# Five projections of a four-layer transformer stack computed with tokens on partitions, their gates multiplied into the weights, and the setup and three orders rearranged

## What is computed

```python
x = x + (cross_attention(ada_ln(x, cond), ctx) @ Wp + bp)              # L0, 64 context keys
x = L1(x)   # evidence attention, router over 3 experts, gate, out_w
# L2
x = x + gate_a * (self_attention(modulate(ln(x))) @ W_proj + b_proj)   # 1024 keys
x = x + (cross_attention(x @ W_qc, ctx) @ W_cproj + b_cproj)
x = x + gate_m * mlp(modulate(ln(x)))                                  # gelu, 1024 hidden
# L3
x = x + gate_sa * (window_attention(modulate(ln(x))) @ w_so + b_so)    # 8 windows of 128
x = x + gate_ca * (topk_attention(modulate(ln(x))) @ w_co + b_co)      # best 16 of 64 keys
x = x + gate_ml * swiglu(modulate(ln(x)))                              # 1024 hidden
```

## Time and profile before

| | us |
|---|---|
| median of 3 runs | 1692.78 |
| lowest, highest | 1691.51, 1701.95 |
| the profiled execution | 1699.16 |
| its span in the trace | 1697.3 |
| PE busy | 1538.0 (91%) |
| DVE busy | 1046.0 (62%) |
| ACT busy | 797.7 (47%) |
| POOL busy | 373.6 (22%) |

### The profile page before, as it was taken

The page is one execution under the profiler, slowest core; times in us unless marked ns, Lnnn a source line. Parts: engine busy times, 40 slices in busy tenths (PEclk is TensorE's granted clock), DMA queues, the critical chain, the costliest instruction groups (busy, mean ns, idle before and its releaser), DMA issues.

```text
span 1697.3 us, 26247 instructions
## 1 busy us (share of the span) xinstructions
PE 1538.0 (91%) x10421; PEld 908.9 (54%) x10421; DVE 1046.0 (62%) x2921; ACT 797.7 (47%) x1264; POOL 373.6 (22%) x418
## 2 busy tenths in 40 slices
PE   5889998999988998877988999899998999887888
PEld 3446564444343856546763657444444476655666
DVE  3363355899627445899357334489982634579953
ACT  1334421688844533335543443148886354233454
POOL 4510006332015110114142000433300600001330
PEclk9989999899999999999999899989999999999899
DMA  9300017221020000000220000632202000000000
GB/s 349 122 1 1 0 42 146 35 37 25 2 75 1 1 1 2 2 1 1 77 86 1 0 0 1 157 49 39 39 2 75 1 1 1 2 2 1 1 1 25
DMA packets 37650, 59.60 MB, mean 35 GB/s; under 512 B 7460, under 2 KB 27079, under 8 KB 36631
## 3 DMA queue, kind: packets, MB, share of 16 engines
q1 hardware_dynamic: 25239, 34.71, 6.1%
q0 software_dynamic: 9568, 15.87, 6.0%
q10 hardware_dynamic: 2720, 7.34, 1.2%
HBM read 42.03 MB, written 2.10 MB: 26 GB/s over the span
## 4 chain that ended last, share of the span: by engine, by line
PE 67%; DVE 17%; issue 6%; ACT 5%; SPq 3%; POOL 2%; DMA 1%; DVEq 0%; ACTq 0%; POOLq 0%
PE ps L963 9%; PE ps L456 9%; PE ps L975 8%; PE ps L1268 4%; PE ps L948 3%; PE ps L843 3%; PE ps L1057 3%; PE ps L1065 3%; DVE rs L2002 2%; PE ps L821 2%; PE ps L578 2%; PE ps L586 2%; DVE mxw L1994 2%; PE ps L1295 2%; DVE taken L2318 2%
## 5 line engine op out<-in xcount | busy, mean ns | idle before, releaser
L2188 DVE TENSOR_REDUCE mm<-ps 128x1 f32<-128x1024 f32 x256 | 310.1, 1223 | 38.7 <-PE ps L948 32.2
L1594 ACT ACTIVATE pt<-ps 128x512 f32<-128x512 f32 x512 | 276.6, 599 | 65.3 <-PE ps L963 47.9
L2430 POOL TENSOR_TENSOR rstd<-ve,minus_half 128x4 f32<-128x4 f32 x32 | 35.7, 1115 | 773.3 <-DVE ve L1881 773.3
L963 PE MATMUL ps<-qx,kx 64*128 64x512 f32 x512 | 192.4, 454 | 2.1 <-DMA qx<-mxT 1.2
L948 PE MATMUL ps<-kx,qx 48*128 48x512 f32 x512 | 191.3, 454 | 0.9 <-DVE mm L2188 0.7
L975 PE MATMUL ps<-pt,v 128*32 128x256 f32 x2048 | 162.4, 398 | 0.0
L963 PEld LDWEIGHTS ps<-qx,kx 64*128 64x128 f32 x512 | 80.8, 188 | 99.8 <-ACT pt L1594 86.4
L2078 DVE TENSOR_TENSOR rlo<-ring,rhi 128x512 fp32r<-128x512 f32 x48 | 33.2, 692 | 128.1 <-ACT ring L1545 128.0
L975 PEld LDWEIGHTS ps<-pt,v 128*32 128x32 f32 x2048 | 43.5, 110 | 88.5 <-ACT pt L1594 61.6
L948 PEld LDWEIGHTS ps<-kx,qx 48*128 48x128 f32 x512 | 77.4, 189 | 23.8 <-issue 15.4
L2476 POOL DMA_DIRECT2D qx<-mxT x64 | 33.0, 523 | 213.5 <-ACT mxT L1586 193.4
(11 more groups left out here) (353 smaller groups left out, 3391.9 us busy)
## 6 DMA issues: line engine op xcount, KB each, us to landing
wm<-in_L_xcond_W_mlp_dram SPq DMA_DIRECT2D x4, 1024.0 KB, 8.6
qx<-q_hi POOLq DMA_DIRECT2D x64, 64.0 KB, 2.6
kx<-k_hi POOLq DMA_DIRECT2D x64, 64.0 KB, 2.7
w3a<-in_L_xcond_w_m_dram SPq DMA_DIRECT2D x2, 2048.0 KB, 8.1
w<-in_L_xcond_e_w_dram SPq DMA_DIRECT2D x6, 512.0 KB, 7.1
w<-in_L_xcond_e_w_dram SPq DMA_DIRECT2D x2, 1536.0 KB, 11.9
s_ada<-in_L_xcond_w_ada_dram ACTq DMA_DIRECT2D x1, 2304.0 KB, 22.0
qx<-q_lo POOLq DMA_DIRECT2D x32, 64.0 KB, 2.5
```

The lines of the kernel that those rows point to most:

```text
L963: pe.matmul(ps[:, bank, :], kx[r, p % 4, kc * P:(kc + 1) * P], qx[r, p % 4, half * 512:(half + 1) * 512], start=True, stop=True).then_inc( ...
L1594: act.activation(pt[:, u % 8, half * 512:(half + 1) * 512], ps[:, bank, :], ACT.Exp, scale=QK_SCALE).then_inc(st_read, 1)
L2188: return dve.tensor_reduce(mm[:, p % 2, e, t:t + 1], place(), X, ALU.max).then_inc(ring_read, 1)
```

## The change

1. A new `projection` on PE makes a block's 512x256 output with tokens on partitions: two bias matmuls (f32r, a 64-partition broadcast column against `row_hl`, 512 columns) and eight fp32 matmuls of 256 columns, straight into the two banks that DVE adds to x. It replaces both parts of `residual` for i = 0, 2, 3, 5, 6; their ACT evictions go.
2. For i = 2, 5, 6 the gate is multiplied into the weight. In the L2 attention PE spreads the three gates over partitions (3 matmuls, banks 5 and 6), ACT copies them to `gates` behind both `high_parts(1, .)`, POOL multiplies wproj, wso and wco (128x512 each) after groups p = 1, 2, 3. PE waits for `gates_ready` at m == 16 (n == -6) of the lead, since the banks are needed again, and for `gates_in` before projection 2.
3. Setup: `load_x(0, 1)` goes right behind `load_x(0, 0)`; five row loads go from POOL to ACT's queue, ahead of the modulation weights; DVE makes statistics and xhat of block 0 after the scales, `s_ctxT`, the gates and 16 small copies into `s_cols`; PE makes the evidence products before the L0 keys and values; two transposes, a copy and a subtraction make `row_hl`, and the first `ln` waits for it (set_dve 14).
4. `kpair` moves to memory of its own and is made in the last MLP of the batch before; at the boundary the two halves of the block-1 query stand before and after `token_scores(0)`.
5. Window loop: DVE takes the maximum before the division, `ln(6, 0)` is at u == 13, `normalise(6, 0)` at u == 12.
6. L3: `up(2)` before `down(0)`, `hidden(2)` before `product_hi(1)`, `centre(6)` before `product_lo(0)`; some semaphores are merged.

```diff
+                def projection(row, k, w, src, bank, sources):
+                    column = row_of[:, N_ROW * b + row:N_ROW * b + row + 1].broadcast_to([64, P])
+                    for j in range(TB // 2):
+                        if j == 0 and sources[0] is not None:
+                            pe.wait_ge(*sources[0])
+                        pe.matmul(ps[:, bank + j, :], column, row_hl[:, :].unsqueeze(1).broadcast_to([64, 2, D]), start=True, stop=False)
+                    for c in range(KC):
+                        if sources[c + 1] is not None:
+                            pe.wait_ge(*sources[c + 1])
+                        for t in range(TB):
+                            ins = pe.matmul(ps[:, bank + t // 2, t % 2 * D:(t % 2 + 1) * D], src[:, k, c, t * P:(t + 1) * P], w[:, c, :],
+                                            start=False, stop=c == KC - 1 and t % 2 == 1)
+                            if c == KC - 1 and t % 2:
+                                ins.then_inc(y_turned, 1)
...
             load_x(0, 0)
+            load_x(0, 1)
...
             load_ra()
-            load_x(0, 1)
...
+            load_rows(act, 24, len(vectors), rows_ld[2])
...
-                residual(2, 0, False, wproj, src=hT, each=(hT_ready, b * 2 * N_HT + 12))
-                linear(6, wproj, 0, hT[:, 1], (hT_ready, b * 2 * N_HT + 14)).then_inc(y_done, 1)
-                residual(2, 0, True)
-                linear(7, wproj, 1, hT[:, 1]).then_inc(y_done, 1)
-                residual(2, 1, True)
+                pe.wait_ge(gates_in, b * 3 + 3)
+                h0 = b * 2 * N_HT + 12
+                projection(R_B_A, 0, wproj, hT, 2, (None, (hT_ready, h0 + 1), (hT_ready, h0 + 2)))
+                projection(R_B_A, 1, wproj, hT, 6, (None, (hT_ready, h0 + 3), (hT_ready, h0 + 4)))
...
                 pe.wait_ge(full_ready, b + 1)
+                for j in range(3):
+                    o = N_ROW * b + R_G_A + j
+                    ins = pe.matmul(ps[:, 5 + j // 2, j % 2 * D:(j % 2 + 1) * D], row_of[:, o:o + 1].broadcast_to([64, P]), row_hl[:, :], start=True, stop=True)
+                ins.then_inc(gates_spread, 1)
                 for n in range(-LEAD, UNITS):
                     (p, u), m = divmod(n, 2 * T), n + LEAD
                     q, at_m = divmod(m, 2 * T)
+                    if m == 2 * T:
+                        pe.wait_ge(gates_ready, b + 1)
...
                 for qk in range(2):
                     high_parts(1, qk)
+                act.wait_ge(gates_spread, b + 1)
+                act.activation(gates[:, 0:2, :], ps[:, 5, :].rearrange("p (j n) -> p j n", j=2), ACT.Copy)
+                act.activation(gates[:, 2, :], ps[:, 6, 0:D], ACT.Copy).then_inc(gates_ready, 1)
...
+                    if p in (1, 2, 3):
+                        if p == 1:
+                            pool.wait_ge(gates_ready, b + 1)
+                            pool.wait_ge(rc1_ld, b * 9 * 16 + 9 * 16)
+                            pool.sem_inc(passed, 1)
+                        w = (wproj, wso, wco)[p - 1]
+                        pool.tensor_tensor(w[:, :, :], w[:, :, :], gates[:, p - 1, :].unsqueeze(1).broadcast_to([P, KC, D]), ALU.mult).then_inc(gates_in, 1)
...
                     if led:
+                        linear(6, wq, 0, hT[:, 1], (hT_ready, b * 2 * N_HT + 2 * (col + 1))).then_inc(q_done, 1)
                         pe.wait_ge(x_final, b * NB)
-                    token_scores(0)
-                    if not led:
+                        token_scores(0)
+                    else:
+                        token_scores(0)
                         linear(6, wq, 0, hT[:, 1], (hT_ready, b * 2 * N_HT + 2 * (col + 1))).then_inc(q_done, 1)
-                    token_scores(1)
-                    if not led:
-                        linear(7, wq, 1, hT[:, 1]).then_inc(q_done, 1)
+                        token_scores(1)
+                    linear(7, wq, 1, hT[:, 1]).then_inc(q_done, 1)
+                    if led:
+                        token_scores(1)
...
                 for u in range(N_UNIT):
+                    if u + 9 < N_UNIT:
+                        window_maximum(u + 9)
                     if u:
                         window_divide(u - 1)
-                    if u + 9 < N_UNIT:
-                        window_maximum(u + 9)
                     if u == 10:
                         build_keys(2)
                     elif u == 11:
                         link(residual(5, 0, 0))
                         statistics(b, 6, 0)
-                    elif u == 13:
+                    elif u == 12:
                         normalise(b, 6, 0)
...
+                up(2)
                 down(0)
-                up(2)
```

More of the change, by code:

```diff
@@ L84 @@
 N_DVE3 = NB * NC_HID - N_POOL3
+YT_ORDER = {1: 0, 4: 1, 7: 2}
+N_ROW = 8
+R_G_A, R_G_SA, R_G_CA, R_BP0, R_B_A, R_BCP, R_B_SA, R_B_CA = range(N_ROW)
 def key_entries(p):
@@ L160, in build @@
         filler = keep("filler", [P, BLK], F32R)
+        row_of = keep("row_of", [64, B * N_ROW], F32R)
+        row_hl = keep("row_hl", [64, D], F32R)
         fr = keep("fr", [P, 2, TB, 4])
@@ L319, in build @@
         wt_half = sem("wt_half")
+        gates_spread, gates_ready, gates_in = sem("gates_spread"), sem("gates_ready"), sem("gates_in")
         wt_ready, wt_read, wm_turned, maxW_ready, ws_ready, wp_exp, wpv_done, wo_ready = (sem(n) for n in (
@@ L542, in _ @@
             as_rows(2, anchor, s_cond)
-            pe.wait_ge(s_kv0_ld, 16)
-            pe.wait_ge(set_dve, 9)
-            for m in range(KC):
-                ins = key(1, m, s_kv0, m, 0)
-            ins.then_inc(set_pe, 1)
-            setup_values(3, s_kv0, 0).then_inc(set_pe, 1)
             pe.wait_ge(mrow_copied, 4)
@@ L568, in _ @@
                 ins.then_inc(set_pe, 1)
+            pe.wait_ge(s_kv0_ld, 16)
+            pe.wait_ge(set_dve, 10)
+            for m in range(KC):
+                ins = key(1, m, s_kv0, m, 0)
+            ins.then_inc(set_pe, 1)
+            setup_values(3, s_kv0, 0).then_inc(set_pe, 1)
+            pe.wait_ge(set_dve, 11)
+            for c in range(KC):
+                ins = pe.transpose(ps[0:64, 0, c * P:(c + 1) * P], s_cols[:, c, :], ident[:, :])
+            ins.then_inc(set_pe, 1)
             pe.wait_ge(set_dve, 8)
@@ new lines, in residual @@
+                def residual(i, k, bank=None, whole=False):
+                    bank = 4 * k if bank is None else bank
+                    for c in range(KC):
+                        if not whole or c == 0:
+                            pe.wait_ge(yT_ready, b * 12 + 2 * (2 * YT_ORDER[i] + k) + (KC if whole else c + 1))
+                        for t in range(TB):
+                            turned = yT7[:, c, :] if (i, k) == (7, 1) else yT[:, k, c, :]
+                            ins = pe.transpose(ps[:, bank + t // 2, t % 2 * D + c * P:t % 2 * D + (c + 1) * P],
+                                               turned[:, t * P:(t + 1) * P], ident[:, :])
+                            if c == KC - 1 and t % 2:
+                                ins.then_inc(y_turned, 1)
@@ L712, in context_attention @@
                     values(3)
-                    residual(step, 0, False, w, (co_ready, u0 + 2), bank=6)
-                    residual(step, 0, True, bank=2)
-                    residual(step, 1, False, w, bank=4, each=(co_ready, u0 + KC))
+                    row = (R_BP0, R_BCP)[i]
+                    projection(row, 0, w, oT, 2, (None, (co_ready, u0 + 2), None))
+                    projection(row, 1, w, oT, 4 + 2 * i, ((co_ready, u0 + 3 - i), (co_ready, u0 + 3), (co_ready, u0 + 4)))
                     ln(step + 1, 0, bank=2 * i)
@@ L845, in expert_out @@
                     ins.then_inc(w2_done, 1)
-                residual(0, 1, True, whole=True)
                 evidence_scores(0)
@@ L894, in _ @@
                     elif n == 17:
-                        residual(1, 0, True, bank=2, whole=True)
+                        residual(1, 0, bank=2, whole=True)
                     elif n == 20:
@@ L1202, in _ @@
                     elif u == 9:
-                        residual(5, 0, False, wso, (wo_ready, u0 + N_UNIT // 2), bank=0)
-                    elif u == 11:
-                        residual(5, 0, True, bank=0, whole=True)
-                    elif u == 14:
+                        projection(R_B_SA, 0, wso, oT, 0, (None, (wo_ready, u0 + N_UNIT // 2), None))
+                    elif u == 13:
                         ln(6, 0, bank=0)
@@ L1895, in pair_keys @@
                 ins.then_inc(kpair_ready, 1)
-            dve.wait_ge(x_ld[0][0], 16)
-            statistics(0, 0, 0)
-            normalise(0, 0, 0)
             def plus_biases(first, bank, lot, lots, chunks):
@@ L1933, in _ @@
             pair_keys(0, 0)
-            normalise(0, 0, 1)
-            dve.wait_ge(set_pe, 10)
-            context_values(0, 3)
-            dve.wait_ge(set_pe, 11)
-            plus_biases(M_HB, 2, 0, E, RH // P)
-            plus_biases(M_HB + MC, 2, E, 1, KC)
```

(13 more changed lines are left out.)

162 lines of the change are left out of this document (76 added, 86 removed).

## The result

The changed kernel takes 1709.2 us (median of 4 runs, 1706.4 to 1712.6) against 1693.7 for the kernel before: ratio 1.007, 95% interval 1.0041 to 1.0099. It is 15.5 us slower where 10.8 faster was forecast, and outside the range. The profiled execution took 1712.6, its span is 1710.7, 13.4 more than before.

A forecast was written before the change was run, and what follows sets the result against it. PE was taken as the main bound, with DMA in the setup and DVE in top-k until its last mask. Twice −1.4 a batch, −4.0 setup and −4.0 boundary gave −10.8, so 1682.0 us from 1692.8; range 1669 to 1696.

The forecast's parts named there:

- the price of the gates' wait: L2 attention lead: PE stands still 4.8 us for the gate copies, costing +4.3 us a batch, between +1 and +9.
- to move forward rather than to come twice: L2 lead: the existing half-clock stretch only shifts earlier after the stall, so the clock adds nothing to the forecast.
- the sum by that rule: Skill's rule on idle gaps: a slow stretch follows the stall, 7.7 us a batch, up to 15 us worse in all.
- Rival B: The stall halves the clock for long in the L2 lead and loop: 17 us a batch, 1707 in all; chance 0.06.
- Rival A: No stall (1673.4 us), or setup, projection, top-k and window at their good ends, −8.5 more; chance 0.25.
- Setup: Before the first query: reordered loads, DVE and PE bring it to 56.9 us, −4.0, between −1 and −5.5.
- I give it nothing, ±0.5: Setup: five row loads put ahead of the modulation weights on ACT's queue were costed at nothing, ±0.5 us.
- 5.75 + 1.0: Setup: time in us from the end of the evidence products to the first query, with block 1's statistics and row_hl.
- Projection 2: i = 2: DVE's second add comes earlier without the transposes, −1.9 us a batch, between −1.2 and −2.5.
- L2 MLP: Second block of i = 3: its transposes between matmuls that bound the stage go whole, −1.2 us a batch.
- Window: Window loop: maximum first −3.4, projection −0.4, query 1.9 later from the earlier ln; −1.4 us a batch, −3.5 to +0.5.
- Top-k: After DVE's last mask PE is the bound and the last projection loses its transposes: −1.2 us a batch, −0.3 to −3.

The follow-up runs named there:

- e2: Changed kernel with 12 filler matmuls on PE before the wait for gates_ready, which stays at m == 16; ratio 0.9994 to the kernel before.
- e3: Kernel before with only a PE wait added at m == 16 of the lead, for ACT's two high_parts copies; ratio 1.0128 to the kernel before.
- e4: Changed kernel with DVE's statistics of block 1 and kpair moved behind row_hl; ratio 1.0027 to the kernel before.
- e8: e5 with the five row loads back on POOL's queue, x of block 1 still early; ratio 0.9952 to the kernel before.
- e5: Changed kernel with the gates_ready wait moved to n == 0 and row_hl ahead of kpair and block 1's statistics; ratio 0.995 to the kernel before.
- e6: e5 with ln(6, 0) back at u == 14 and normalise(6, 0) at u == 13; ratio 0.9904 to the kernel before.
- e12: The changed kernel unaltered, timed again on another chip; ratio 1.0069 to the kernel before.
- e1: Changed kernel with PE's wait for gates_ready moved from m == 16 to n == 0; ratio 0.9945 to the kernel before.
- e11: e6 with the five row loads back on POOL's queue and load_x(0, 1) back behind load_ra; ratio 0.9884 to the kernel before, 1679.9 us.

## Why the prediction was wrong, step by step

**The step that failed is the price of the gates' wait, and in it the clock.** The place, the cause and the length were right: copies behind high_parts, PE there 4 us too early, 3.70 and 4.21 us of idle against 4.8 worked out. I had the earlier trace rows in hand, which showed the lower level behind an idle time of 4.74 us, and then took the stretch of lower level "to move forward rather than to come twice". It did neither: it began in the wait itself and ran on past the place of the old one, at 0.50 in all seven stretches of 4 us from 304 to 332. e2 gives the terms: of 21 us, 8 are delay (8.6 forecast) and 13 are clock (nothing forecast). The Trainium skill says of such gaps that they bring the lower level ("TensorE: Matmul & The Clock Gate", section "Why this matters for your kernels"). The two leads agree with it, and the sum by that rule, up to 15 us worse than mine, was near the mark. With 19.3 in place of 8.6, the forecast of −10.8 becomes −0.1. The 13.5 us from there to the +13.4 between the traces are setup +3.1, top-k +4.6, and some 6 in small terms: L1 in both batches, the window, the boundary and the places where the clock differs.

How regular the price is shows in four traces with such a wait (the changed kernel twice, e3, e4): the waits were 3.70, 3.97, 3.07 and 3.80 us in batch 0 and 4.21, 4.19, 3.72 and 2.67 in batch 1, and the lead grew each time by the wait and 5.4 us in batch 0, and by the wait and 5.9 to 6.0 in batch 1. The extra did not depend on the wait's length between 2.7 and 4.2 us.

**Rival B** was the mechanism, with a chance of 0.06. Its own working gave 17 us a batch for the wait and 1707 in all; measured were 9.1 and 10.2 a batch and 1709, so its total was right for reasons partly wrong: the wait exceeded its forecast by less than B had it, and the rest of the sum came out worse, which made up for it by luck. Its argument "Against" (a mean clock of 0.97 over the loop) was no argument: a mean over 176 us hides 10 us at half, and it is these 10 us that make the 0.97.

**Rival A** has a slip in its sum: by the forecast's own figures the good ends are 0.6 + 1.8 + 2.1 = 4.5 a batch and not 3.5, so −10.5 in place of −8.5. It bears on nothing here, since none of these ends came.

**Setup: −4.0 forecast, −0.9 measured.** The order of DVE and PE did what was worked out: the evidence products ended 4.2 us earlier (50.98; 50.2 was forecast). Two terms failed. "I give it nothing, ±0.5" for the five row loads: 2.8 us on the modulation products, and 3.7 between e8 and e5. And "5.75 + 1.0" for the chain behind, which took 9.05: statistics and kpair stood between the keys and row_hl (e4: 2.0 us, 0.8 of it the first ln at half clock, 1.94 against 1.10). This chain is the larger part of what the setup missed, 2.3 of 3.1. The 1.3 us for x ahead of s_an were about right in size: 0.95 in the two pairs above.

**Projection 2: −1.9 a batch forecast**, −1.6 and −1.4 to the query, and −3.6 and −2.4 to its last product. The difference is the clock: in the kernel before it stood at 0.50 in 500 to 504 us, where this query ran, and at 1.00 in the changed one. That the shorter wait in front (1.23 us for 1.62) gave this slow stretch back is not shown: in batch 1 the clock fell there in the changed kernel too, and its query took 5.19 us.

**L2 MLP: −1.2 forecast**, +1.9 and −3.6 measured. Both are the clock again: in batch 0 it fell near 556 now and not before, in batch 1 before and not now. Like with like the stage takes 42.80 us now and 43.61 before with the fall, and 40.02 and 40.91 without it. So the change is worth 0.8 to 0.9 a batch in this stage, where the transposes alone had been put at 1.2 (96 of their 256 records are left in all, as forecast), and a fall of the clock here costs 2.7 to 2.8.

**Window: −1.4 forecast, −0.9 measured**, by its parts: 0.58 per unit from the maximum first (0.57 forecast), but in five units and not six, since one of the waits had been 0.44 before too: −2.9 for −3.4. The projection gave −0.3 (0.4 forecast), and +2.3 is left for the ln a unit too early (1.9 and 0.5 of rounding forecast). e6 takes 1.4 of this back.

**Top-k: −1.2 a batch forecast, 0 measured** behind the last mask. PE now waits 0.78 us for ACT's `up` where the transposes had stood:

```profile
832.23 0.73 PE L1292 MATMUL ps<-hs,w3a_hi 128*128 128x512 f32 x2 [0.78 <-ACT up L1405]
```

The step that failed is "after it PE is the bound": ACT is, by a little. Ahead of the mask batch 0 lost 2.1 us; what is seen of it is a mask on DVE that took 3.43 us in place of 1.99 beside POOL (below) and more stretches of lower clock.

**Batch boundary: −4.0 forecast, −3.2 measured**, with the order and the 1.17 for the second scores as worked out; later scores still run at 2.09 (897.11).

**Bias matmuls:** 0.65 us for a pair (673.03 to 673.68 in the window loop) against 0.6 at most in the sum. **POOL's products** of gates and weights: 1.3 us each, hidden.

## What to carry to other kernels

A wait of PE costs its length and then the time until the clock is back: in the lead of this kernel waits of 2.7 to 4.2 us cost 8.5 to 10.2, and filling one with useless matmuls won back two thirds. It is not so at every wait (see the next section), so the price is to be looked for in the trace. So a new wait on PE is placed by its first real user (here six units later, at no cost), and its producer goes ahead of long waits on its own engine (here 22 us of idle time on ACT stood in front of two copies). A row that shows half clock behind an idle time is a price to put into the sum, not into the range, and a few small loads put ahead of large ones on a queue that is waited for are not free either.

## What the runs showed of the hardware that I had not expected

The lower clock level outlasts its cause: in the changed kernel it lasts from 304 to past 332 us, with PE busy at least 3.3 of every 4 us. Why the slow stretch before (10 us, with a wait of 0.37 the longest in the lead) arises at all, and why the new one lasts three times as long, stays open. Nor is a given idle time always followed by it: in the MLP near 550 us PE has the same waits in both kernels (1.50 or 1.38, then 0.96 and 1.63 us; busy 1.44 of 4 us), and the clock stays at 1.00 in the one and falls to 0.50 in the other. In batch 1 it is the other way about.

```profile
550.00:554.00 4.00, 3.86 (x21) 3.30 (x22) 1.18 (x3) 2.67 (x5) 0.00 (x0) 1.00 0.02 4
```

(The kernel before, behind the idle time; the first line under e12 is the same work.) Such dips cost 2.7 to 2.8 us here and 1.7 near 620 us (the window projections, 76.67 us against 74.99 in the other batch). They come again at the same place in a second execution of the same kernel, and lie elsewhere when something earlier has moved (near 545 us and not at 620 in e1). Their sum moves the time of one and the same kernel: over the 25 executions of the kernel before that were timed beside e1 to e4, the time goes from 1692 up to 1704 us while the mean granted clock goes from 0.965 down to 0.953. So a difference of a few us between two of these kernels can be made of such dips. That e4, e6 and e11 moved by more than their edits explain fits this; no run shows it for them.

DVE behaves in places as if it waited for POOL. The top-k stage's mask on DVE (128x1024) takes 1.22 us alone. In nine cases of the two traces a POOL product was running when the mask began, or began with it; the mask then took 1.96 to 3.43 us and ended each time 1.07 to 1.09 us after that product. In the three cases where the mask began 0.10 to 0.12 us before the product it took its 1.22. `kpair` took 2.41 us beside POOL's `vw` at the boundary, the first of its two instructions ending 0.14 us after POOL's, and 0.48 in its new place. A small POOL operation did not do it: beside the rstd of 128x4 at 56.06 `kpair` took 0.48 too. Below are the changed kernel's DVE, then its POOL at the same moment:

```profile
788.16 3.43 DVE L2360 SCALAR_TENSOR_TENSOR prob<-taken,prob 128x1024 f32<-128x1024 f32 x1
```

```profile
788.16 2.36 POOL L2578 TENSOR_TENSOR hTlo<-hT,hs 128x1024 fp32r<-128x1024 f32 x1 [6.41 <-ACT hT L1405]
```
